# Sixteen tiles of y loaded ahead of the second pass, twelve of them into other rings

## The chip, the cores and the metric

One core of a Trainium2 chip runs the kernel. The metric is the device time of one execution in microseconds (us), the median of several runs. Lower is better.

## What is computed

x is a tensor of 2048 images x 512 channels x 8 x 8, float32. Two layers follow each other, each on a group norm of its input (32 groups of 16 channels, statistics per image):

```python
x = x + L0(_gn(x))      # L0: each channel's 8x8 block is mixed by one 64x64 matrix, plus a bias
x = x + L1(_gn(x))

def L1(x):
    h = sign(batchnorm(x, bn1_gamma, bn1_beta))          # over images and positions, per channel
    bw = sign(conv_w) * scale_of(conv_w)
    h = conv3x3(h, bw, groups=16)
    h = batchnorm(h, bn2_gamma, bn2_beta) + x
    return where(h > 0, h, prelu_a * h)
```

The two batch norms need sums over all 2048 images before anything can go on. They cut the kernel into three passes over the data.

## The kernel before, in words

**Tiles.** x is taken in B = 128 units of 16 images: 128 partitions (4 images x 32 groups) x 4096 floats, 2 MB. Pass 1 makes y, the group-normed input of the second layer, and writes it to y_scratch in DRAM. Pass 2 reads y again in T2 = 256 tiles of 32 images x 128 channels (partitions are channels there), takes the signs, convolves, and writes the integer sums h, packed two to a word, to h_scratch. Pass 3 (T3 = 128 tiles) reads y and h and writes out.

**Engines.** Each engine runs its own list of instructions, written out by hand; semaphores join them. Every transfer is issued by SyncE (the block at L313), in the order of its list. `rounds` (L281) writes out the first tiles of a pass, then a hardware loop of four tiles a turn, then four tiles more. `i, c` is the round and the place in it; tile t is `SLOTS * i + c`.

**Pass 1.** Per unit and quarter TensorE turns ring_x (L1002), ScalarE copies the turned values to ring_gT (L577) and takes mean and square of x with ring_g as a place to throw the values (L584, L590), TensorE mixes (L1016, L1019; semaphore mixed), VectorE adds x and puts z in ring_z (L764, evicted) and counts it (L773, z_counted), GpSimd normalises z into ring_y (L481, y_done), and SyncE stores ring_y (store_y, L338).

**Between the passes.** VectorE, TensorE and GpSimd turn the sums into the scale and shift of the first batch norm, bn1 (L805 to L831, bn1_ready). The pair has to change its layout from 32 groups to 128 channels, so SyncE writes it to DRAM (L372, bn1_out) and reads it back (L375, bn1_in), 4 KB each. The first sign (L632) waits for bn1_in. SyncE has by then loaded the first four tiles of y into ring_x (L365), between the stores of y of units 125 and 126.

**Pass 2.** ScalarE signs a tile (take_sign, L626, two activations L632), VectorE packs two halves into one frame (L840), TensorE convolves with 18 matmuls (L1084), ScalarE unpacks two tiles later (L637, L643) into one of four word slots, VectorE counts h (L848) and every 16 tiles sums up (L855), SyncE stores the word slot (store_h, L380, L383). A y tile is 1 MB in two transfers of 512 KB (load_y2, L354, L359), rows of 1 KB; an h tile is one transfer of 512 KB. There are four y slots, all in ring_x:

```python
            def pass2(i, c):
                t = SLOTS * i + c
                if until(i, c, T2 - SLOTS):
                    sp.wait_ge(signed, 2 * t + 2)
                    load_y2(i, c + SLOTS)
                if from_round(i, c, 3):
                    store_h(i, c - 3)
```

ring_z, ring_y, ring_g and ring_gT aren't used in pass 2; pass 3 uses them for y and h from its first loads on (load_3, L396).

Of the kernel before, what the change touches and what calls it, by code (L numbers as in the profile page):

```python
# [18 lines left out]
SIDE = 8  # L19
J = C // P  # L20
NQ = 4
# [3 lines left out]
FU = NQ * SL  # L25
UNIT = NQ * (P // GROUPS)
BANK = 512
PAIRS = GC // 2
HEAD = TAIL = 4
SLOTS = 4  # L30
# [4 lines left out]
IMG = 16  # L35
# [21 lines left out]
def two_layer_kernel(nc, x, w0, b0, conv_w, g1, be1, g2, be2, prelu_a, ident_in, quarter_in, clif_in, pick_in, out):  # L57
    N = x.shape[0]
    B = N // UNIT
    T2 = (B // 2) * J  # L60
# [13 lines left out]
    y_chan = y_dram.rearrange("b (m k c f) -> b k c m f", m=4, k=J, c=P)  # L74
# [3 lines left out]
    with ExitStack() as ctx:  # L78
        def sb(name, shape, dt=F32):
            return ctx.enter_context(nc.sbuf_tensor(name, shape, dt))  # L80

        def sem(name):
            return ctx.enter_context(nc.semaphore(name))

        ring_x = sb("ring_x", [P, SLOTS, FU])
        ring_z = sb("ring_z", [P, 2, FU])
        ring_y = sb("ring_y", [P, 2, FU])
        ring_g = sb("ring_g", [P, SLOTS, SL])
        ring_gT = sb("ring_gT", [P, SLOTS, SL])
        late = sb("late", [P, 2, 2048])  # L90
        early = sb("early", [P, GC * P])
# [84 lines left out]
        def y2_slot(s):  # L176
            return ring_x[:, s // 2, 2048 * (s % 2):2048 * (s % 2) + 2048]

        def word_slot(s):
            return ring_x[:, 2, 1024 * s:1024 * s + 1024].bitcast(I32)  # L180

# [13 lines left out]
        def relu_slot(m):  # L195
            return late[:, m // 4, BANK * (m % 4):BANK * (m % 4 + 1)]

        def sum_bank(m):
            return h_acc[m // 2][:, BANK * (m % 2):BANK * (m % 2 + 1)]

# [24 lines left out]
        x_squared = sem("x_squared")  # L225
# [6 lines left out]
        mixed = sem("mixed")  # L232
        evicted = sem("evicted")
        z_counted = sem("z_counted")
# [5 lines left out]
        y_stored = [sem(f"y_stored{s}") for s in range(2)]  # L240
# [9 lines left out]
        bn1_in = sem("bn1_in")  # L250

        y2_loaded = [sem(f"y2_loaded{s}") for s in range(SLOTS)]
        signed = sem("signed")
        packed = sem("packed")
        conv_done = sem("conv_done")
# [25 lines left out]
        def rounds(eng, body, total, head=HEAD):  # L281

            loops = (total - head - TAIL) // SLOTS
            for c in range(head):
                body(0, c)
            with eng.Fori(0, loops) as i:
                for c in range(head, head + SLOTS):
                    body(i, c)
            for c in range(head, head + TAIL):
                body(loops, c)  # L290

        def from_round(i, c, n):

            return not (isinstance(i, int) and SLOTS * i + c < n)

        def until(i, c, n):

            return not (isinstance(i, int) and SLOTS * i + c >= n)

        def row(ap, b):  # L300
            if isinstance(b, int):
                return ap[b]
            one = ap[bass.ds(b, 1)]
            return one.rearrange("a p f -> (a p) f") if len(one.shape) == 3 else one.rearrange(
                "a p n f -> (a p) n f")
# [8 lines left out]
        def _(sp):  # L314
# [23 lines left out]
            def store_y(i, c):  # L338
                b = SLOTS * i + c
                sp.wait_ge(y_done, 4 * b + 4)  # L340
                sp.dma_start(row(y_unit, b), ring_y[:, c % 2, :]).then_inc(y_stored[c % 2], 16)
# [11 lines left out]

            def load_y2(i, c):  # L354

                s = c % SLOTS
                pair = 2 * (i + c // J)
                for e in range(2):
                    sp.dma_start(y2_slot(s)[:, 1024 * e:1024 * (e + 1)].rearrange("p (m f) -> p m f", m=4),  # L359
                                 row(y_chan[:, c % J], pair + e)).then_inc(y2_loaded[s], 16)  # L360

            sp.wait_ge(evicted, 4 * (B - 2))
            sp.wait_ge(y_stored[0], 16)
            sp.wait_ge(y_stored[1], 16)
            for c in range(SLOTS):  # L365
                load_y2(0, c)
            loops1 = (B - SLOTS) // SLOTS
            store_y(loops1, SLOTS - 2)
            store_y(loops1, SLOTS - 1)

            sp.wait_ge(bn1_ready, 1)
            sp.dma_start(bn1_dram.rearrange("(q j) s -> q (j s)", j=GC),  # L372
# [3 lines left out]
                         allow_slow_non_contiguous=True).then_inc(bn1_in, 16)  # L376
            for s in range(2):
                sp.wait_ge(y_stored[s], 16 * (B // 2))

            def store_h(i, c):  # L380
                t = SLOTS * i + c
                sp.wait_ge(unpacked, t + 1)
                sp.dma_start(row(h_chan[:, c % J], i + c // J),  # L383
                             word_slot(c % SLOTS).rearrange("p (m f) -> p m f", m=4)).then_inc(h_stored[c % SLOTS], 16)

            def pass2(i, c):
                t = SLOTS * i + c
                if until(i, c, T2 - SLOTS):
                    sp.wait_ge(signed, 2 * t + 2)
                    load_y2(i, c + SLOTS)  # L390
                if from_round(i, c, 3):
                    store_h(i, c - 3)

            rounds(sp, pass2, T2, 2 * HEAD)

            def load_3(i, c):  # L396

# [161 lines left out]
        def _(act):  # L559
# [65 lines left out]

            def take_sign(i, c):  # L626
                t, s = SLOTS * i + c, c % SLOTS
                act.wait_ge(y2_loaded[s], 32 * (i + c // SLOTS + 1))
                if from_round(i, c, 2):
                    act.wait_ge(packed, t - 1)  # L630
                for e in range(2):
                    act.activation(  # L632
                        sign_slot(c % 2)[:, e].rearrange("p (a n b) -> p n a b", a=SIDE, n=IMG),
                        y2_slot(s)[:, 1024 * e:1024 * (e + 1)].rearrange("p (n a b) -> p n a b", n=IMG, a=SIDE),
                        ACT.Sign, bias=bn1_c[:, c % J, 1:2], scale=bn1_c[:, c % J, 0:1]).then_inc(signed, 1)

            def unpack(i, c):  # L637
# [13 lines left out]
                if from_round(i, c, 2):  # L651
                    unpack(i, c - 2)

            rounds(act, pass2, T2, 2 * HEAD)
            last = (T2 - SLOTS) // SLOTS
            unpack(last, SLOTS - 2)
            unpack(last, SLOTS - 1)
# [33 lines left out]
        def _(dve):  # L691
# [56 lines left out]
            for n in range(NQ):  # L748
                dve.tensor_scalar(rank_rhs[:, n, :].rearrange("p (r f) -> p r f", f=S),
                                  part.unsqueeze(1).to_broadcast([P, BANK // S, S]), pick[:, 5 + n:6 + n], None,  # L750
                                  ALU.mult).then_inc(rank_ready, 1)
# [15 lines left out]
            def z_stat(i, c, j):  # L767
# [3 lines left out]
                dve.wait_ge(evicted, 4 * (SLOTS * i + c) + j + 1)  # L771
                for r in range(PAIRS):
                    last = dve.bn_stats(z_tup[:, s, j, 2 * r:2 * r + 2, :].rearrange("p h t -> p (h t)"),  # L773
# [69 lines left out]
            def h_stat(i, c):  # L843
# [3 lines left out]
                for q in range(4):  # L847
                    last = dve.bn_stats(h_tup[:, c % J, c // J, q, :], parts[:, BANK * q:BANK * (q + 1)])  # L848
                last.then_inc(h_counted, 1)
# [142 lines left out]
        def _(pe):  # L992
            def turn(i, c, j):
# [5 lines left out]
                if from_round(i, c, 1) or j >= 2:  # L999
                    pe.wait_ge(gT_done, step - 1)  # L1000
                for r in range(PAIRS):
                    last = pe.transpose(psT[:, j % 2, P * r:P * (r + 1)],  # L1002
# [8 lines left out]
            def product(i, c, j):  # L1011
# [3 lines left out]
                for h in range(2):  # L1015
                    pe.matmul(psV[:, j % 2, BANK * h:BANK * (h + 1)], rank_lhs[:, c % 2, :], rank_rhs[:, j, :],  # L1016
                              start=True, stop=False)
# [126 lines left out]
```

## Time and profile before

| | us |
|---|---|
| runs, median of 3 | 4591.73 (4591.44 to 4593.64) |
| the profiled execution, its own time | 4591.19 |
| its span in the profile | 4589.1 |
| TensorE matmuls busy | 4297.1 |
| VectorE busy | 4173.0 |
| ScalarE busy | 3861.6 |
| GpSimd busy | 1476.0 |

The profile is of one execution; all times in it count from the start of its span. Pass 1 ends near 1751, pass 2 runs from 1761 to about 2805. The transfers moved 1612.18 MB. Busy time is not the same as being the limit: an engine can be busy 90% of the time and still wait for something each turn. The DMA share is the mean busy share of the 16 DMA engines; in this profile it goes a little over 1 where they are full. "To landing" is the time from the issue of a transfer to its last byte. SPq is the queue of SyncE, that is, the time it spends on issuing transfers.

### The profile page before, as it was taken

The page shows a single profiled execution, that of the slowest core. Times are in us where ns is not written, and L with a number is a line of the kernel's source. Part 1 is how long each engine was busy: PE and PEld are TensorE (multiplying, and loading weights), DVE is VectorE, ACT ScalarE, POOL GpSimd, SP SyncE. Part 2 cuts the span into 40 slices and gives each one's busy share as a digit, 9 for nine tenths or more (in the row PEclk, how much of TensorE's full clock was granted, in tenths as well). Part 3 has the DMA queues.
Part 4 walks back from the last instruction along what each step waited for, and adds up shares of the span by engine and source line. Part 5 has one row for each costly group of instructions (what it writes and reads, how often), then busy time and mean ns, then how long its engine had stood idle before and what let it go on. Part 6 is the DMA issues. An engine that isn't in the chain of part 4 may idle for free.

```text
span 4589.1 us, 82259 instructions
## 1 busy us (share of the span) xinstructions
PE 4297.1 (94%) x21948; PEld 2702.5 (59%) x21948; DVE 4173.0 (91%) x9963; ACT 3861.6 (84%) x5517; POOL 1476.0 (32%) x3480
## 2 busy tenths in 40 slices
PE   6999999999999997999999995999999999999998
PEld 6999999999999994444444442444444444444443
DVE  6999999999999997999899987999999999999998
ACT  7999999999999995888888885777777777777776
POOL 3888888888888883000000000000000000000000
PEclk9999999999999998999999998999999999999999
DMA  5888888888888889999999997999999999999998
GB/s 198 317 318 320 316 316 323 314 319 322 316 317 318 320 302 315 385 385 385 385 385 385 385 385 289 383 389 388 389 387 386 390 387 389 387 388 387 388 387 308
DMA packets 686230, 1612.18 MB, mean 351 GB/s; under 512 B 30002, under 2 KB 423986, under 8 KB 620658
## 3 DMA queue, kind: packets, MB, share of 16 engines
q1 hardware_dynamic: 686194, 1611.76, 95.7%
q8 instruction: 16, 0.26, 0.0%
q14 instruction: 20, 0.16, 0.0%
HBM read 940.55 MB, written 671.10 MB: 351 GB/s over the span
## 4 chain that ended last, share of the span: by engine, by line
PE 51%; SPq 20%; ACT 11%; DVE 9%; issue 8%; DMA 1%; DVEq 0%; ACTq 0%; POOL 0%
PE psV L1019 17%; SPq L359 12%; PE psT L1002 10%; DVE ring_x L958 8%; SPq L383 7%; PE psT L1104 5%; PE psV L1016 5%; PE psT L1106 5%; PE psV L1106 4%; PE psV L1104 4%; ACT ring_y L678 3%; ACT ring_z L678 3%; ACT ring_g L584 2%; PE psV L1100 1%; ACT late L668 1%
## 5 line engine op out<-in xcount | busy, mean ns | idle before, releaser
L1019 PEld LDWEIGHTS psV<-W0T,ring_gT 128*128 128x128 f32 x8192 | 1077.0, 192 | 33.7
L1019 PE MATMUL psV<-W0T,ring_gT 128*128 128x128 f32 x8192 | 1080.2, 275 | 0.0
L773 DVE BATCH_NORM_STATS2 early<-ring_z 128x6 f32<-128x128 f32 x4096 | 822.6, 274 | 0.0
L764 DVE SCALAR_TENSOR_TENSOR ring_z<-psV,x_r,ring_x 128x1024 f32<-128x1024 f32 x512 | 657.3, 1284 | 117.6 <-DVE early L773 76.9
L668 ACT ACTIVATE late<-ring_x,minus_b 128x512 f32<-128x512 f32 x1024 | 639.6, 707 | 0.9 <-PE psV L1106 0.9
L848 DVE BATCH_NORM_STATS2 h_tup<-ring_x 128x6 f32<-128x512 uint16 x1024 | 630.7, 678 | 0.5
L632 ACT ACTIVATE ring_x<-ring_x,bn_c 128x1024 f16<-128x1024 f32 x512 | 604.1, 1230 | 31.0 <-DMA bn_c<-bn_scratch 31.0
L481 POOL TENSOR_SCALAR ring_y<-ring_z,u_r,u_nm 128x1024 f32<-128x1024 f32 x512 | 605.7, 1199 | 35.6 <-POOL gn L500 35.6
L590 ACT ACTIVATE ring_g<-ring_x,x_ms 128x1024 f32<-128x1024 f32 x512 | 585.2, 1143 | 0.0
L577 ACT ACTIVATE ring_gT<-psT 128x1024 f32<-128x1024 f32 x512 | 523.7, 1023 | 49.2 <-PE psT L1002 23.7
L678 ACT ACTIVATE ring_y<-ring_y,gnb 128x512 f32<-128x512 f32 x512 | 368.1, 801 | 211.2 <-DVE ring_x L958 175.7
L1084 PE MATMUL psT<-late 128*128 128x448 f16 (+3 forms) x2304 | 480.5, 364 | 67.0 <-DVE late L840 66.9
L1002 PE MATMUL psT<-ident,ring_x 128*128 128x128 f32 x4096 | 538.8, 275 | 3.9 <-ACT rank_lhs L596 0.4
L584 ACT ACTIVATE ring_g<-ring_x 128x1024 f32<-128x1024 f32 x512 | 536.9, 1049 | 0.0
L678 ACT ACTIVATE ring_z<-ring_z,gnb 128x512 f32<-128x512 f32 x512 | 368.1, 801 | 190.2 <-DVE ring_x L958 190.2
L1106 PE MATMUL psT<-late,early 128*128 128x512 f32 x1024 | 523.8, 593 | 0.0
L1084 PE MATMUL psV<-late 128*128 128x448 f16 (+3 forms) x2304 | 475.5, 362 | 31.4 <-DVE late L840 31.4
L976 DVE SCALAR_TENSOR_TENSOR ring_x<-ring_x,bn_q,psV 128x512 f32<-128x512 f32 x512 | 374.3, 744 | 117.5 <-PE psV L1106 90.3
L1002 PEld LDWEIGHTS psT<-ident,ring_x 128*128 128x128 f32 x4096 | 458.9, 141 | 26.3 <-ACT rank_lhs L596 25.5
L1084 PEld LDWEIGHTS psT<-late 128*128 128x128 f16 x2304 | 216.2, 98 | 330.7 <-issue 88.8
L1016 PE MATMUL psV<-early,rank_lhs 128*128 128x512 bf16 x1024 | 389.1, 380 | 19.6 <-ACT ring_gT L577 5.5
L840 DVE SCALAR_TENSOR_TENSOR late<-ring_x 128x1024 f16<-128x1024 f16 x256 | 312.9, 1222 | 102.5 <-ACT ring_x L632 92.8
(153 smaller groups left out, 5682.8 us busy)
## 6 DMA issues: line engine op xcount, KB each, us to landing
ring_x<-in_x SPq DMA_DIRECT2D x128, 2048.0 KB, 8.8
y_scratch<-ring_y SPq DMA_DIRECT2D x128, 2048.0 KB, 12.8
ring_x<-y_scratch SPq DMA_DIRECT2D x512, 512.0 KB, 7.6
out<-ring_x SPq DMA_DIRECT2D x256, 1024.0 KB, 14.4
h_scratch<-ring_x SPq DMA_DIRECT2D x256, 512.0 KB, 7.8
ring_y<-y_scratch SPq DMA_DIRECT2D x128, 1024.0 KB, 8.1
ring_z<-y_scratch SPq DMA_DIRECT2D x128, 1024.0 KB, 8.2
ring_g<-h_scratch SPq DMA_DIRECT2D x64, 1024.0 KB, 12.2
```

The lines of the kernel that those rows point to most:

```text
L481: pool.tensor_scalar(ring_y[:, c % 2, :].rearrange("p (r n s) -> p n r s", r=GC, n=NQ)[:, j], ring_z[:, c % 2, SL * j:SL * (j + 1)].rearra ...
L584: act.activation(ring_g[:, 2 * (j % 2), :], ring_x[:, s, SL * j:SL * (j + 1)], ACT.Copy, scale=-1.0 / (SL * ROOT), accum_out=x_ms[:, s, 0, ...
L668: act.activation(relu_slot(m), t_slot(c % 2)[:, m], ACT.Relu, bias=minus_b2[:, ch:ch + 1], scale=-1.0).then_inc(relu_done, 1)
L678: last = act.activation(v, v, ACT.Identity, bias=gnb[:, s, e, 0, n:n + 1], scale=gnb[:, s, e, 1, n:n + 1])
L764: dve.scalar_tensor_tensor(out=ring_z[:, c % 2, cols], in0=psV[:, j % 2, :], scalar=x_r[:, s, j:j + 1], in1=ring_x[:, s, cols], op0=ALU.mu ...
L773: last = dve.bn_stats(z_tup[:, s, j, 2 * r:2 * r + 2, :].rearrange("p h t -> p (h t)"), ring_z[:, c % 2, SL * j + 2 * S * r:SL * j + 2 * S ...
L848: last = dve.bn_stats(h_tup[:, c % J, c // J, q, :], parts[:, BANK * q:BANK * (q + 1)])
L1002: last = pe.transpose(psT[:, j % 2, P * r:P * (r + 1)], ring_x[:, s, SL * j + P * r:SL * j + P * (r + 1)], ident[:, :])
L1016: pe.matmul(psV[:, j % 2, BANK * h:BANK * (h + 1)], rank_lhs[:, c % 2, :], rank_rhs[:, j, :], start=True, stop=False)
L1019: last = pe.matmul(psV[:, j % 2, P * r:P * (r + 1)], ring_gT[:, j, P * r:P * (r + 1)], W0T[:, :], start=False, stop=(r % 4 == 3))
L1084: last = pe.matmul(sums[:, IMG * a.start:IMG * a.stop, b.start:b.stop], conv_wT[:, c % J, tap, :], rows[:, IMG * (a.start + dy):IMG * (a.s ...
L1106: pe.matmul(sum_bank(m), diag[:, 8 * (c % 2) + m, :], relu_slot(m), start=False, stop=True).then_inc(combined, 1)
```

## The change

SyncE loads tiles 0 to 3 as before. Behind them it loads tiles 4 and 5 into ring_g once the last square of x is done, 6 and 7 into ring_gT once the last product is done, then stores units 126 and 127, loads tiles 8 to 11 into ring_z once the last z is counted and stored, does the two bn1 transfers, and loads tiles 12 to 15 into ring_y. In the pass, tile t = 0 to 3 is followed by the load of tile t + 16 into its slot in ring_x, tiles 4 to 15 by none, and from tile 16 on t is followed by t + 4, as before. The twelve early tiles have semaphores of their own.

```diff
+AHEAD = 16
...
+        def y2_place(i, c):
+
+            if not (isinstance(i, int) and SLOTS <= SLOTS * i + c < AHEAD):
+                return y2_slot(c % SLOTS)
+            n = SLOTS * i + c - SLOTS
+            if n < SLOTS:
+                return (ring_g if n < 2 else ring_gT)[:, 2 * (n % 2):2 * (n % 2) + 2, :].rearrange("p s f -> p (s f)")
+            return (ring_z if n < 2 * SLOTS else ring_y)[:, :, :].rearrange("p s f -> p (s f)")[
+                :, 2048 * (n % SLOTS):2048 * (n % SLOTS) + 2048]
...
+        y2_early = [sem(f"y2_early{t}") for t in range(SLOTS, AHEAD)]
...
             def load_y2(i, c):
 
-                s = c % SLOTS
+                early = isinstance(i, int) and SLOTS <= SLOTS * i + c < AHEAD
+                loaded = y2_early[SLOTS * i + c - SLOTS] if early else y2_loaded[c % SLOTS]
                 pair = 2 * (i + c // J)
                 for e in range(2):
-                    sp.dma_start(y2_slot(s)[:, 1024 * e:1024 * (e + 1)].rearrange("p (m f) -> p m f", m=4),
-                                 row(y_chan[:, c % J], pair + e)).then_inc(y2_loaded[s], 16)
+                    sp.dma_start(y2_place(i, c)[:, 1024 * e:1024 * (e + 1)].rearrange("p (m f) -> p m f", m=4),
+                                 row(y_chan[:, c % J], pair + e)).then_inc(loaded, 16)
 
             sp.wait_ge(evicted, 4 * (B - 2))
-            sp.wait_ge(y_stored[0], 16)
-            sp.wait_ge(y_stored[1], 16)
+            for s in range(2):
+                sp.wait_ge(y_stored[s], 16 * (AHEAD // J))
             for c in range(SLOTS):
                 load_y2(0, c)
             loops1 = (B - SLOTS) // SLOTS
+            sp.wait_ge(x_squared, NQ * B)
+            load_y2(1, 0)
+            load_y2(1, 1)
+            sp.wait_ge(mixed, NQ * B)
+            load_y2(1, 2)
+            load_y2(1, 3)
             store_y(loops1, SLOTS - 2)
             store_y(loops1, SLOTS - 1)
+            sp.wait_ge(z_counted, NQ * B)
+            for c in range(SLOTS):
+                load_y2(2, c)
 
             sp.wait_ge(bn1_ready, 1)
...
             for s in range(2):
                 sp.wait_ge(y_stored[s], 16 * (B // 2))
+            for c in range(SLOTS):
+                load_y2(3, c)
...
             def pass2(i, c):
                 t = SLOTS * i + c
                 if until(i, c, T2 - SLOTS):
-                    sp.wait_ge(signed, 2 * t + 2)
-                    load_y2(i, c + SLOTS)
+                    if not from_round(i, c, SLOTS):
+                        sp.wait_ge(signed, 2 * t + 2)
+                        load_y2(i, c + AHEAD)
+                    elif from_round(i, c, AHEAD):
+                        sp.wait_ge(signed, 2 * t + 2)
+                        load_y2(i, c + SLOTS)
                 if from_round(i, c, 3):
                     store_h(i, c - 3)
 
-            rounds(sp, pass2, T2, 2 * HEAD)
+            rounds(sp, pass2, T2, AHEAD)
...
             def take_sign(i, c):
                 t, s = SLOTS * i + c, c % SLOTS
-                act.wait_ge(y2_loaded[s], 32 * (i + c // SLOTS + 1))
+                if not from_round(i, c, SLOTS):
+                    act.wait_ge(y2_loaded[s], 32)
+                elif not from_round(i, c, AHEAD):
+                    act.wait_ge(y2_early[t - SLOTS], 32)
+                else:
+                    act.wait_ge(y2_loaded[s], 32 * (i + c // SLOTS + 2 - AHEAD // SLOTS))
...
-            rounds(act, pass2, T2, 2 * HEAD)
+            rounds(act, pass2, T2, AHEAD)
```

SyncE's order from the end of pass 1 to the first stores of h, before (a row is one kind of transfer, "waits" names the semaphores ahead of it; ring_x<-y_scratch are y tiles, two transfers each):

```order
L341 DMA y_scratch<-ring_y 128x4096 [waits y_done] x4
L359 DMA ring_x<-y_scratch 128x4x256 [waits y_stored1,y_stored0,evicted]
L359 DMA ring_x<-y_scratch 128x4x256 x7
L341 DMA y_scratch<-ring_y 128x4096 [waits y_done] x2
L372 DMA bn_scratch<-bn_q 32x32 [waits bn1_ready]
L375 DMA bn_c<-bn_scratch 128x4x2 [waits bn1_out]
L359 DMA ring_x<-y_scratch 128x4x256 [waits signed,y_stored1,y_stored0]
L359 DMA ring_x<-y_scratch 128x4x256
```

Between the last two y stores and the bn1 transfers nothing stands.

The same place in the changed kernel (the line numbers are its own; L372 is load_y2, L353 store_y, L394 and L397 the bn1 transfers):

```order
L353 DMA y_scratch<-ring_y 128x4096 [waits y_done] x4
L372 DMA ring_x<-y_scratch 128x4x256 [waits y_stored1,y_stored0,evicted]
L372 DMA ring_x<-y_scratch 128x4x256 x7
L372 DMA ring_g<-y_scratch 128x4x256 [waits x_squared]
L372 DMA ring_g<-y_scratch 128x4x256 x3
L372 DMA ring_gT<-y_scratch 128x4x256 [waits mixed]
L372 DMA ring_gT<-y_scratch 128x4x256 x3
L353 DMA y_scratch<-ring_y 128x4096 [waits y_done] x2
L372 DMA ring_z<-y_scratch 128x4x256 [waits z_counted]
L372 DMA ring_z<-y_scratch 128x4x256 x7
L394 DMA bn_scratch<-bn_q 32x32 [waits bn1_ready]
L397 DMA bn_c<-bn_scratch 128x4x2 [waits bn1_out]
```

Eight transfers now stand ahead of the last two y stores, and eight more ahead of the bn1 transfers.

Behind the bn1 transfers, before the hardware loop of pass 2, in the changed kernel:

```order
L372 DMA ring_y<-y_scratch 128x4x256 [waits y_stored1,y_stored0]
L372 DMA ring_y<-y_scratch 128x4x256 x7
L372 DMA ring_x<-y_scratch 128x4x256 [waits signed]
L372 DMA ring_x<-y_scratch 128x4x256
L372 DMA ring_x<-y_scratch 128x4x256 [waits signed]
L372 DMA ring_x<-y_scratch 128x4x256
L372 DMA ring_x<-y_scratch 128x4x256 [waits signed]
L372 DMA ring_x<-y_scratch 128x4x256
L372 DMA ring_x<-y_scratch 128x4x256 [waits signed]
L372 DMA ring_x<-y_scratch 128x4x256
L407 DMA h_scratch<-ring_x 128x4x256 [waits unpacked] x13
```

Sixteen transfers of y stand ahead of the first store of h where eight stood, and then thirteen stores of h follow with no load between them.

## Rows read from the trace of the kernel before

**Rows 1.** The page's chain that ended last, whole span, by engine and by line
```profile
PE 51%; SPq 20%; ACT 11%; DVE 9%; issue 8%; DMA 1%; DVEq 0%; ACTq 0%; POOL 0%
PE psV L1019 17%; SPq L359 12%; PE psT L1002 10%; DVE ring_x L958 8%; SPq L383 7%; PE psT L1104 5%; PE psV L1016 5%; PE psT L1106 5%; PE psV L1106 4%; PE psV L1104 4%; ACT ring_y L678 3%; ACT ring_z L678 3%; ACT ring_g L584 2%; PE psV L1100 1%; ACT late L668 1%
```

**Rows 2.** Busy time by windows in the second pass
```profile
core 0: us, PE busy (x) PEld busy (x) DVE busy (x) ACT busy (x) POOL busy (x), PEclk, DMA share, GB/s
1850.00:2750.00 900.00, 820.51 (x3972) 372.50 (x3971) 818.23 (x1221) 723.03 (x662) 0.00 (x0) 1.00 1.09 385
...
1850.00:1900.00 50.00, 46.22 (x226) 21.05 (x225) 44.61 (x63) 40.15 (x38) 0.00 (x0) 1.00 1.09 385
...
2650.00:2700.00 50.00, 45.02 (x218) 20.40 (x219) 45.52 (x70) 40.36 (x38) 0.00 (x0) 1.00 1.09 385
```

**Rows 3.** Who waited for whom, 1850 to 2750 us
```profile
engine line waited for: us in total, times, longest us
ACT ring_x L643 <- DMA h_scratch<-ring_x: 171.0, 212, 1.0
```

**Rows 4.** ScalarE's timeline, end of pass 1 and start of pass 2
```profile
start us, us, engine line op out<-in xcount [idle before <-releaser]
1711.47 1.15 ACT L590 ACTIVATE ring_g<-ring_x,x_ms 128x1024 f32<-128x1024 f32 x1
...
1761.19 6.90 ACT L632 ACTIVATE ring_x<-ring_x,bn_c 128x1024 f16<-128x1024 f32 x6 [31.04 <-DMA bn_c<-bn_scratch]
...
1772.05 2.36 ACT L632 ACTIVATE ring_x<-ring_x,bn_c 128x1024 f16<-128x1024 f32 x2
...
1775.62 2.36 ACT L632 ACTIVATE ring_x<-ring_x,bn_c 128x1024 f16<-128x1024 f32 x2
...
1785.41 1.02 ACT L643 ACTIVATE ring_x<-psT 128x1024 int32<-128x1024 f32 x1 [0.29 <-PE psT L1084]
...
1800.77 2.36 ACT L632 ACTIVATE ring_x<-ring_x,bn_c 128x1024 f16<-128x1024 f32 x2
...
1857.77 2.36 ACT L632 ACTIVATE ring_x<-ring_x,bn_c 128x1024 f16<-128x1024 f32 x2
```

**Rows 5.** Timelines of VectorE and TensorE in the first tiles of pass 2
```profile
1778.34 1.23 DVE L840 SCALAR_TENSOR_TENSOR late<-ring_x 128x1024 f16<-128x1024 f16 x1
...
1803.33 1.22 DVE L840 SCALAR_TENSOR_TENSOR late<-ring_x 128x1024 f16<-128x1024 f16 x1
...
1781.64 7.30 PE L1084 MATMUL psT<-late 128*128 128x512 f16 x36
1788.78 7.30 PE L1084 MATMUL psV<-late 128*128 128x512 f16 x36
```

**Rows 6.** The chain of waits between the passes, 1726 to 1762 us
```profile
1730.42 0.91 PE psV L1019 x8
...
1738.12 3.08 DVE early L773 x16
...
1757.66 0.19 DVE bn_q L831
1757.87 1.35 DMA bn_scratch<-bn_q
1759.24 1.93 DMA bn_c<-bn_scratch
```

**Rows 7.** SyncE's timeline: transfers issued between the passes (start, time to issue)
```profile
1726.60 0.33 SPq L341 DMA_DIRECT2D y_scratch<-ring_y  x1
...
1727.05 12.74 SPq L359 DMA_DIRECT2D ring_x<-y_scratch  x8
...
1740.22 1.02 SPq L341 DMA_DIRECT2D y_scratch<-ring_y  x1
...
1751.13 0.36 SPq L341 DMA_DIRECT2D y_scratch<-ring_y  x1
...
1763.65 11.70 SPq L359 DMA_DIRECT2D ring_x<-y_scratch  x8
```

**Rows 8.** Busy time by windows between the passes
```profile
1732.00:1734.00 2.00, 2.00 (x18) 1.91 (x16) 1.96 (x9) 0.00 (x0) 1.92 (x7) 1.00 0.85 196
1734.00:1744.00 10.00, 0.14 (x2) 0.00 (x0) 7.76 (x30) 0.00 (x0) 9.00 (x20) 0.75 1.10 357
1744.00:1750.00 6.00, 0.00 (x0) 0.00 (x0) 3.37 (x7) 0.00 (x0) 5.84 (x13) 0.50 1.07 427
1750.00:1752.00 2.00, 0.18 (x1) 0.18 (x2) 1.63 (x5) 0.00 (x0) 1.11 (x1) 0.50 0.12 49
...
1758.00:1764.00 6.00, 0.00 (x0) 0.00 (x0) 0.40 (x1) 2.81 (x3) 6.00 (x11) 0.50 0.05 1
1764.00:1766.00 2.00, 0.97 (x3) 0.43 (x4) 1.02 (x2) 2.00 (x3) 2.00 (x4) 0.50 0.53 95
...
1768.00:1770.00 2.00, 2.00 (x6) 0.69 (x5) 0.00 (x0) 0.10 (x1) 0.13 (x1) 0.55 1.09 351
```

**Rows 9.** L359 issued 1726-1740 and at 1763.65; L383 issued 1774-1790: time to landing
```profile
DMA to landing us min/median/max: 8.6/10.2/11.0
...
DMA to landing us min/median/max: 3.9/3.9/3.9
...
DMA to landing us min/median/max: 6.2/6.9/9.4
```

**Rows 10.** VectorE's sums over four tiles, groups of 1850 to 2780 us
```profile
L855 DVE BATCH_NORM_AGGREGATE h_agg<-h_tup 128x2 f32<-128x48 f32 x112 | 27.7, 319 | 0.0
```

More of the change, by code:

```diff
@@ L633, in take_sign @@
                         sign_slot(c % 2)[:, e].rearrange("p (a n b) -> p n a b", a=SIDE, n=IMG),
-                        y2_slot(s)[:, 1024 * e:1024 * (e + 1)].rearrange("p (n a b) -> p n a b", n=IMG, a=SIDE),
+                        y2_place(i, c)[:, 1024 * e:1024 * (e + 1)].rearrange("p (n a b) -> p n a b", n=IMG, a=SIDE),
                         ACT.Sign, bias=bn1_c[:, c % J, 1:2], scale=bn1_c[:, c % J, 0:1]).then_inc(signed, 1)
```

## The prediction

> **What bounds the kernel now.** I read the page first. Its chain of waits [rows 1] names TensorE and, next, the issuing queue of SyncE with the y loads of the second pass (L359); so the second pass hangs on transfers, not on an engine. The windows view of it [rows 2] shows why: over 900 us the 16 DMA engines are at a share of 1.09 and move a constant 385 GB/s, while TensorE is busy for 820.51 us and VectorE for 818.23, both about 91%. The waits of the same stretch [rows 3] say where it is felt: ScalarE's unpack (L643) waits 171.0 us, in 212 pieces, for the store of h that frees its word slot. Nobody waits for a y load. One tile loads 1.049 MB and stores 0.524 MB; 1.573 MB at 385 GB/s is 4.09 us.
>
> The pass doesn't start at that pace. In ScalarE's timeline [rows 4] tile 0 is signed from 1761.19 (the last bn1 transfer has landed), tile 3 at 1772.05, tile 4 at 1775.62, tile 11 at 1800.77 and tile 25 at 1857.77. So tiles 4 to 11 come every (1800.77 - 1775.62) / 7 = 3.59 us, later ones every (1857.77 - 1800.77) / 14 = 4.07. The 3.57 is the engines' own pace: VectorE packs tile 4 at 1778.34 and tile 11 at 1803.33 without a gap, 25.0 / 7 = 3.57, and 36 matmuls, two tiles, start 7.14 us apart [rows 5]. **The most that any early load can give is thus 4.07 - 3.57 = 0.50 us per tile**, and only while it lasts.
>
> Between the passes the chain [rows 6] runs through VectorE's last counts, GpSimd's and VectorE's small bn1 steps, and from 1757.87 two small transfers of 1.35 and 1.93 us, which SyncE issues and which hold back the first sign. SyncE's own timeline [rows 7]: the store of unit 125 at 1726.60, eight loads (four tiles) from 1727.05 to 1739.79, the stores of units 126 and 127 at 1740.22 and 1751.13, then bn1. The windows [rows 8] show the DMA engines full until 1750 (357 GB/s in loads alone, 427 while the store is in), nearly idle in 1750 to 1752, and idle from 1758 to 1764. The idle time is what the change wants to fill. It is short, some 10 us, and four tiles take 4.19 MB / 0.357 = 11.7 us. Where SyncE's rows stand in the new order is shown with the change.
>
> **The change part by part.** Four parts matter.
>
> (a) Eight tiles (1,0) to (2,3) stand in SyncE's order ahead of the bn1 transfers, the first four ahead of the last two y stores as well. Their own waits end early: the last square ends at 1712.6 [rows 4], the last product at 1731.3 and the last count at 1741.2 [rows 6], all before SyncE gets to the loads behind them. SyncE doesn't run ahead freely: its eight issues took 12.74 us in a full queue [rows 7], and loads landed 8.6 to 11.0 us after issue there, against 3.9 in an empty queue [rows 9]. So I take one line of transfers, served in turn. Before, the four tiles have drained at about 1744, when the rate rises [rows 8]. Add four tiles, 11.7: 1755.7. The two stores, 2.10 MB each at 427 GB/s, 4.9 each: 1765.5 (the last became ready at 1751.1, so it costs no wait). Four more tiles, 11.7: 1777.2. bn1 has been ready since 1757.9 [rows 6]; its write lands 1.35 after what lies before it, its read 1.93 and a few hundredths later: the first sign at 1780.5 instead of 1761.2. **Cost: 19.3 us**, on the path, because every engine waits for bn1 here. Bounds: if the loads ran at the 427 GB/s of the store's window and the bn1 write overlapped the last load, 14.1 (2 x 1.9 and 1.35 less); if each change between loads and stores cost about a microsecond more, as the 196 GB/s of 1732 to 1734 suggests [rows 8], 22. I take 19.3, from the rates of the same kinds of transfer.
>
> That a queue is served in turn is also in the Trainium skill, page "DMA: Bandwidth & Descriptors", section "Two DMAs through the same engine are not ordered": within one queue of an engine descriptors start in order. It speaks against this change. The loads' landing times of 8.6 to 11.0 us agree; whether a 4 KB transfer is held up too, no row of before shows.
>
> (b) Tiles 12 to 15 are issued after the bn1 read and before anything of pass 2, and then tiles 16 to 19, each after a sign; only then the store of h of tile 0. Before, four tiles stood there. Now 8.39 MB at 0.357 take 23.5 us. The first load before was issued at 1763.65 and the rate was full at 1766 [rows 7, 8], 2.3 later; now the issue is 1.6 before the first sign, so the flow starts at T + 0.8 (T is the first sign) and ends at T + 24.3. The store of tile 0, 0.524 MB at 385 GB/s, lands at T + 25.7. ScalarE's unpack of tile 4, which needs that slot, started at T + 24.2 [rows 4]. **Cost: 1.5 us**, on the path, since VectorE had no slack behind it [rows 5]. Bounds 0 and 5 (the 351 GB/s of a single 2 us window [rows 8], and a landing as late as the 6.9 us median of the first four h stores [rows 9]).
>
> (c) Gain. Tiles 4 to 15 now find their data there, and no load is issued while they run, because the later loads go only into the four slots of ring_x. So tile 16 stands where tile 4 stood before: four tiles in store, queue empty. Until there 12 tiles go at 3.57 instead of 12 tiles that, later on, cost 4.07. **Gain: 12 x 0.50 = 6.0 us.** The queue is idle for most of that: 12 stores, 6.3 MB, 16 us of 43. Bounds: 8.0 if the whole 16 tiles count; 3.3 if VectorE's sums after tile 19 (8 BN_AGGR of 319 ns and a copy, 2.7 us [rows 10]) aren't hidden.
>
> (d) The rest costs nothing. The waits on x_squared, mixed and z_counted are over when SyncE arrives; the store of unit 126 goes out at about 1751 instead of 1740, but nothing needs ring_y until pass 2's loads. ScalarE has 16 tiles written out instead of 8: the same activations. Pass 3 is untouched.
>
> Sum: 19.3 + 1.5 - 6.0 = +14.8. The profiled execution took 4591.19 us (span 4589.1), 0.5 below the median of 4591.73, so it may stand for the runs: 4591.73 + 14.8 = **4606.5 us**, 0.32% slower. About 0.2%, 9.2 us, is what a measurement of this kernel can tell from no change.
>
> A second rule of that page, section "Specifications", puts HBM at some 358 GB/s per core. By it the later tiles would take 1.573 / 0.358 = 4.39 us, the gain would be 9.9 and the sum +10.9. The trace disagrees, with 385 GB/s over 900 us, and the measurement decides.
>
> **Rivals.**
> *The small transfers pass the queue.* The bn1 write then lands 1.35 us after its issue. SyncE gets to it when the last load is issued, 8.6 to 11.0 us before 1777.2, so about 1768; the first sign comes at 1771 to 1772, 10 us late. But the loads still have to drain: the h store of tile 0 lands behind the same bytes, only 4.1 us sooner than in the forecast (1777.2 + 23.5 + 1.4 = 1802.1), and the unpack of tile 4, ready at 1771.5 + 24.2, waits 6.4 us for it. Sum 10.3 + 6.4 - 6.0 = +10.7: 4602. For it: the small size. Against it: SyncE's one queue.
> *Bytes decide.* If pass 2 lasted as long as its bytes at 385 GB/s from the first sign, the eight tiles that are no longer loaded in it would save 8 x 2.72 = 21.8 us: 19.3 + 1.5 - 21.8 = -1, 4591, no change. The trace of before speaks against it: tiles 4 to 11 don't beat 3.57 us although DMA is not yet the limit. The Trainium skill's same page, "Rules for kernel authors", says to issue a transfer early and wait for it late; by that rule alone the early loads are free, which is the saving of this case.
> *Another steady pace* (the faster side). If the 4.07 us came not from the DMA engines but from how loads and stores follow each other in SyncE's line, a start with full slots and no store outstanding could keep a better rhythm. Place: tiles 24 to 255. It decides from a pace 0.10 us shorter on, since (14.8 + 9.2) / 232 = 0.10; with 3.57 plus 2.7 / 16 for the sums, 3.74, it would be 4606.5 - 232 x 0.33 = 4530. Against it: a share of 1.09 and 385 GB/s, the same at the start and at the end of the 900 us [rows 2].
> *A deeper stall of the h stores*: (b) at its upper end and (a) at 21: 4612.
>
> **How the numbers follow.** Forecast 0.72; passing the queue 0.06; bytes decide 0.09; another pace 0.08; deeper stall 0.05. The forecast's bounds give +6 (14.1 + 0 - 8.0) to +23.7 (22 + 5 - 3.3); not all ends meet, and I take +6 to +22, with 0.06 of its 0.72 below +9.2. The range is 4597 to 4614: it leaves out bytes decide and another pace (0.17) and little else. Slower by over 0.2%: 0.66 + 0.06 + 0.05 = 0.77. Within: 0.09 + 0.06 = 0.15. Faster: 0.08.
>
> **What would show it.** In the profile of the changed kernel: the bn1 write issued at about 1768 or later and landing only near 1778, not 1.35 us after 1757.9; the first sign (L632's counterpart) near 1780; a wait of 1 to 5 us at the unpack of tile 4; tiles 4 to about 23 every 3.57 us; a window of some 25 us with the DMA share well below 1; then 385 GB/s and 4.07 us per tile to the end, and a third pass of the same length. A first sign before 1775, or a later pace below 4.0 us, would prove me wrong.

## The result, and the profile after

| | before | changed |
|---|---|---|
| median of the runs, us | 4591.66 | 4608.47 (4607.25 to 4609.88) |
| ratio, 95% interval | | 1.0036 (1.0025 to 1.0046) |
| span of the profiled execution | 4589.1 | 4605.2 |

The change costs 16.8 us, 0.37%. Forecast were 14.8 us and 4606.5. Lines of code below are those of the changed kernel: L372 is load_y2, L394 and L397 the bn1 transfers, L407 the store of h, L665 the sign, L676 the unpack, L873 VectorE's pack.

SyncE's timeline between the passes (start, time to issue), which answers to [rows 7]:

```profile
1726.51 12.77 SPq L372 DMA_DIRECT2D ring_x<-y_scratch  x8
1739.72 5.35 SPq L372 DMA_DIRECT2D ring_g<-y_scratch  x4
1745.12 6.16 SPq L372 DMA_DIRECT2D ring_gT<-y_scratch  x4
1751.32 1.89 SPq L353 DMA_DIRECT2D y_scratch<-ring_y  x2
1753.26 19.61 SPq L372 DMA_DIRECT2D ring_z<-y_scratch  x8
1772.92 1.41 SPq L394 DMA_DIRECT2D bn_scratch<-bn_q  x1
1780.32 0.38 SPq L397 DMA_DIRECT2D bn_c<-bn_scratch  x1
1780.80 8.44 SPq L372 DMA_DIRECT2D ring_y<-y_scratch  x8
1789.29 12.15 SPq L372 DMA_DIRECT2D ring_x<-y_scratch  x8
1801.48 36.02 SPq L407 DMA_DIRECT2D h_scratch<-ring_x  x13
```

SyncE is stuck in the issue of the tiles for ring_z when bn1 becomes ready (1757.9 before). It gets to the bn1 write at 1772.92. The chain of waits of the changed kernel, the place that answers to [rows 6] (start, duration):

```profile
1772.92 7.38 DMA bn_scratch<-bn_q
1780.30 0.02 issue
1780.32 1.92 DMA bn_c<-bn_scratch
1782.24 0.02 issue
1782.26 2.38 ACT ring_x L665 x2
```

The write takes 7.38 us, not 1.35. It lands at 1780.30, right behind the last load, which was issued at 1771.46 and took 8.7 us to land: it doesn't pass the loads that were issued before it. The read, alone in the queue, takes 1.92 as before. ScalarE's timeline, the start of pass 2, against [rows 4]:

```profile
1782.26 6.90 ACT L665 ACTIVATE ring_x<-ring_x,bn_c 128x1024 f16<-128x1024 f32 x6 [52.66 <-DMA bn_c<-bn_scratch]
...
1803.11 2.36 ACT L665 ACTIVATE ring_x<-ring_gT,bn_c 128x1024 f16<-128x1024 f32 x2
1809.84 1.02 ACT L676 ACTIVATE ring_x<-psT 128x1024 int32<-128x1024 f32 x1 [4.37 <-PE psT L1117]
1810.76 2.36 ACT L665 ACTIVATE ring_x<-ring_gT,bn_c 128x1024 f16<-128x1024 f32 x2
...
1829.85 2.36 ACT L665 ACTIVATE ring_x<-ring_y,bn_c 128x1024 f16<-128x1024 f32 x2
...
1840.56 2.36 ACT L665 ACTIVATE ring_x<-ring_x,bn_c 128x1024 f16<-128x1024 f32 x2
...
1888.43 1.02 ACT L676 ACTIVATE ring_x<-psV 128x1024 int32<-128x1024 f32 x1 [0.69 <-DMA h_scratch<-ring_x]
```

The first sign is 21.1 us late. The row at 1809.84 is the unpack of tile 4, which waits 4.37 us. The profile names TensorE as the releaser, but with fewer loads ahead of the first store of h this unpack starts 23.9 us after the first sign (the last but one experiment), which would be 1806.2. The other semaphore of the wait is that of the first store of h, which was issued at 1801.48 and took 8.3 us to land: 1809.8, just when the unpack starts. Tile 7 is signed at 1810.76 and tile 13 at 1829.85, 3.18 us a tile: ScalarE works off what TensorE has already done, and makes up 2.3 us. Then tiles go at 3.57 to tile 16 (1840.56). Only at 1888.43 does a wait for a store of h come back.

Windows between and in the passes (the last three columns are the granted clock, the DMA share and GB/s), against [rows 2, 8]:

```profile
1744.00:1756.00 12.00, 1.22 (x4) 1.00 (x4) 5.69 (x15) 0.00 (x0) 8.89 (x12) 0.50 1.10 349
...
1780.00:1782.00 2.00, 0.00 (x0) 0.00 (x0) 0.00 (x0) 0.00 (x0) 0.00 (x0) 0.50 0.15 5
...
1812.00:1840.00 28.00, 26.43 (x135) 12.85 (x134) 26.85 (x38) 27.14 (x26) 0.00 (x0) 1.00 0.50 170
1840.00:1850.00 10.00, 10.00 (x52) 4.89 (x51) 10.00 (x16) 9.35 (x9) 0.00 (x0) 1.00 0.55 179
...
1870.00:2770.00 900.00, 823.29 (x3993) 375.00 (x3991) 821.67 (x1232) 725.13 (x663) 0.00 (x0) 1.00 1.09 385
```

The DMA engines are full while everybody waits for bn1, and at about half load for the 38 us in which the tiles loaded ahead are worked off. At 385 GB/s they would have moved 8.1 MB more in these 38 us, which is 21 us of their time. After that the pass is what it was, 385 GB/s at a share of 1.09. Pass 2 ends 15.4 us late: the bn2 write that follows it is issued here, before and after.

```profile
2828.21 0.37 SPq L415 DMA_DIRECT2D bn_scratch<-bn_c  x1
```

```profile
2843.61 0.37 SPq L443 DMA_DIRECT2D bn_scratch<-bn_c  x1
```

The 0.7 us left of the 16.1 between the spans lie behind the bn2 write, and are not explained.

### The profile page after: what moved, and what is told of

Read it like the earlier page. It is cut to its first block, busy times and chain, and to the rows that moved or that the text cites. A ratio compares the mean times of both kernels' runs of the same rounds, so it can differ in the third digit from the quotient of the medians.

```text
span 4605.2 us, 81925 instructions
## 1 busy us (share of the span) xinstructions
PE 4257.1 (92%) x21692; PEld 2702.9 (59%) x21948; DVE 4171.2 (91%) x9963; ACT 3861.8 (84%) x5517; POOL 1479.6 (32%) x3480
## 4 chain that ended last, share of the span: by engine, by line
PE 21%; SPq 19%; POOL 18%; DVE 15%; issue 15%; ACT 8%; DMA 1%; POOLq 1%; DVEq 1%; ACTq 0%
SPq L372 12%; DVE ring_x L991 8%; SPq L407 6%; POOL ring_y L509 6%; PE psT L1137 5%; PE psT L1139 5%; PE psV L1137 4%; PE psV L1139 4%; DVE early L806 4%; ACT ring_y L711 3%; ACT ring_z L711 3%; POOL u_r L523 2%; POOL x_r L485 2%; DVE ring_z L797 2%; PE psV L1133 1%
## 5 line engine op out<-in xcount | busy, mean ns | idle before, releaser
L665 ACT ACTIVATE ring_x<-ring_x,bn_c 128x1024 f16<-128x1024 f32 x488 | 575.8, 1230 | 52.8 <-DMA bn_c<-bn_scratch 52.7
L873 DVE SCALAR_TENSOR_TENSOR late<-ring_x 128x1024 f16<-128x1024 f16 x256 | 312.5, 1221 | 120.0 <-ACT ring_x L665 110.8
L1139 PE MATMUL psV<-late,early 128*128 128x512 f32 x768 | 392.2, 592 | 0.0
```

Of the source, the lines that this page charges most:

```text
L665: act.activation(sign_slot(c % 2)[:, e].rearrange("p (a n b) -> p n a b", a=SIDE, n=IMG), y2_place(i, c)[:, 1024 * e:1024 * (e + 1)].rearr ...
L1139: pe.matmul(sum_bank(m), diag[:, 8 * (c % 2) + m, :], relu_slot(m), start=False, stop=True).then_inc(combined, 1)
```

## The experiments

The theory after the result: while the DMA engines are the limit of pass 2, only the bytes that they don't move count, whatever the reason (no load issued, an empty queue). (All transfers of y and h in pass 2 are of 512 KB, so bytes can't be told from the number of transfers here.) Three rivals: the late bn1 is a loss by itself (A); a small transfer is held up by the full DMA engines, whichever queue it comes from (B); the pace of 4.07 us is a rhythm of SyncE's list (C).

The ratios compare each kernel with the kernel before, run beside it. The median of the kernel before was 4591.66 us beside the change and 4592.51 to 4592.71 beside the experiments, so a difference of 1 to 2 us between an experiment and the change isn't much more than this drift. Where it matters the time of the bn2 write in the profiles is given too.

**The bn1 transfers issued by ScalarE**

```diff
-            sp.wait_ge(bn1_ready, 1)
-            sp.dma_start(bn1_dram.rearrange("(q j) s -> q (j s)", j=GC),
...
-            sp.wait_ge(bn1_out, 16)
-            sp.dma_start(bn1_c[:, :, :], bn1_dram.rearrange("(k p) s -> p k s", p=P),
...
+            act.wait_ge(bn1_ready, 1)
+            act.dma_start(bn1_dram.rearrange("(q j) s -> q (j s)", j=GC),
...
+            act.wait_ge(bn1_out, 16)
+            act.dma_start(bn1_c[:, :, :], bn1_dram.rearrange("(k p) s -> p k s", p=P),
             act.wait_ge(bn1_in, 16)
```

> The change, but the two bn1 transfers are issued by ScalarE, so they don't stand in SyncE's line. Theory (bytes in line): what costs is the bytes that stand ahead of the first store of h; the first sign then comes near 1763 us, not 1782, but the unpack of tile 4 still waits for a store that lands near 1804, some 18 us instead of 4. Only the few us in which the DMA engines idle around bn1 come back: about 4603. Rival A (the late bn1 is itself the loss): nearly all of the 21 us come back, 4588. Rival B (a transfer of another queue waits behind the full DMA engines all the same): first sign after 1775, 4607.

Measured: 4606.2 us, ratio to before 1.0029 (1.0018 to 1.0041). ScalarE's timeline of this kernel (L659 is the sign, L670 the unpack):

```profile
1758.58 0.36 ACTq L675 DMA_DIRECT2D bn_scratch<-bn_q  x1
1763.98 0.40 ACTq L678 DMA_DIRECT2D bn_c<-bn_scratch  x1
1771.07 6.91 ACT L659 ACTIVATE ring_x<-ring_x,bn_c 128x1024 f16<-128x1024 f32 x6 [40.26 <-DMA bn_c<-bn_scratch]
...
1807.13 1.02 ACT L670 ACTIVATE ring_x<-psT 128x1024 int32<-128x1024 f32 x1 [12.97 <-issue]
```

The first sign comes 11.2 us sooner than in the change, and 8.5 us of that are lost again at the unpack of tile 4, with 12.97 us of waiting. A falls: of the 21 us 2.3 came back by the medians, and in the profiles the bn2 write is 0.7 us earlier. B is half right: beside full DMA engines the two small transfers took 5.4 and 7.1 us, against 1.35 and 1.93 alone [rows 6]. The first sign came 8 us later than the theory had it (1763), the total 3.2 us above its 4603 and nearer to B's 4607. As a small transfer is slow in a queue of its own too, the 7.38 us of the change don't tell the turn in SyncE's queue from the full engines.

**All twelve tiles behind the bn1 transfers**

```diff
-            sp.wait_ge(x_squared, NQ * B)
-            load_y2(1, 0)
...
-            for c in range(SLOTS):
-                load_y2(2, c)
...
-            for c in range(SLOTS):
-                load_y2(3, c)
+            for n in range(1, 4):
+                for c in range(SLOTS):
+                    load_y2(n, c)
```

> The change, but tiles 4 to 11 are loaded behind the bn1 transfers too, with tiles 12 to 15. Theory (bytes in line): the first sign is back at 1761, but sixteen tiles (16 x 3.0 us) stand ahead of the first store of h, which lands near 1812; the unpack of tile 4 waits about 27 us and the total is 4611, as slow as the change. Rival A (the late bn1 is the loss): 4591.7 + 4 - 6, about 4590.

Measured: 4611.76 us, ratio 1.0043 (1.0026 to 1.0060). Its first sign and its unpack of tile 4:

```profile
1761.11 6.90 ACT L657 ACTIVATE ring_x<-ring_x,bn_c 128x1024 f16<-128x1024 f32 x6 [31.01 <-DMA bn_c<-bn_scratch]
...
1812.85 1.02 ACT L668 ACTIVATE ring_x<-psT 128x1024 int32<-128x1024 f32 x1 [28.04 <-issue]
```

The clearest of the runs: 4611 and 27 us were expected, 4590 by rival A. The first sign comes when it did before (1761.11), and the kernel is the slowest of all. The same twelve tiles stand ahead of the first store of h instead of bn1, and the wait is 28.04 us there.

**Four tiles instead of twelve**

```diff
-AHEAD = 16
+AHEAD = 8
...
-            sp.wait_ge(z_counted, NQ * B)
-            for c in range(SLOTS):
-                load_y2(2, c)
...
-            for c in range(SLOTS):
-                load_y2(3, c)
```

> Eight tiles ahead instead of sixteen: only tiles 4 to 7, into ring_g and ring_gT, in the place where the change has its first four. Theory: the line is 12 us longer, bn1 waits for the last y store, first sign near 1769.5 (+8); the first h store stands behind no more than before, so unpack of tile 4 doesn't wait; four tiles at 0.5 us are gained: 4597 to 4598. Rival A expects the same here; if the gain is 2.7 us a tile (bytes decide), 4589.

Measured: 4599.39 us, ratio 1.0016 (1.0006 to 1.0026). The loss shrinks to 6.9 us, 1.4 us more than the upper end of what was expected. For four tiles used up in a row 2.7 us a tile (4589) is excluded. The first sign came at 1771.83, 2 us later than expected, because the bn1 write stood 11.0 us behind two y stores:

```profile
1758.90 0.33 SPq L391 DMA_DIRECT2D bn_scratch<-bn_q  x1
1769.94 0.39 SPq L394 DMA_DIRECT2D bn_c<-bn_scratch  x1
```

**The same sixteen tiles, used up slowly.** The sixteen slots are kept in turn, and one load in about nine is left out, each time one for a slot outside ring_x, until four slots are left. `LOAD[t]` is the tile loaded after tile t, and from tile SPREAD (112) on t is followed by t + 4 in the four slots.

```diff
                 if until(i, c, T2 - SLOTS):
-                    if not from_round(i, c, SLOTS):
-                        sp.wait_ge(signed, 2 * t + 2)
-                        load_y2(i, c + AHEAD)
-                    elif from_round(i, c, AHEAD):
+                    if from_round(i, c, SPREAD):
                         sp.wait_ge(signed, 2 * t + 2)
                         load_y2(i, c + SLOTS)
+                    elif t in LOAD:
+                        sp.wait_ge(signed, 2 * t + 2)
+                        load_y2(0, LOAD[t])
```

> The change, but the loads that are left out are not those after tiles 4 to 15 in a row: one in about nine is left out (after tiles 8, 20, 26, 35, 48, 53, 62, 71, 80, 89, 100, 111), so that the DMA engines never idle and the engines' own pace (3.57, 3.74 with the sums) never binds. Theory (bytes decide once the DMA engines are kept full): each tile loaded ahead is then worth 1.049 MB / 385 GB/s = 2.72 us instead of 0.5, 12 x 2.2 = 26 us better than the change: 4582, 10 us faster than before. Rival C (the 4.07 us pace comes from the rhythm of SyncE's list, or the gain is bound to tiles and not to bytes): 4605 to 4609.

Measured: 4587.87 us, ratio 0.9990 (0.9981 to 1.0000). Nothing ahead of the first sign differs from the change (it came at 1782.92), and the kernel is 20.6 us faster than the change, about 4.6 us faster than before, at the edge of the interval. C as it was put, 4605 or more, falls. Three of its windows:

```profile
1810.00:1860.00 50.00, 46.47 (x229) 21.58 (x228) 43.25 (x61) 41.96 (x39) 0.00 (x0) 1.00 1.09 384
1860.00:1910.00 50.00, 47.73 (x239) 22.85 (x238) 48.83 (x76) 43.60 (x42) 0.00 (x0) 1.00 1.09 385
...
2450.00:2750.00 300.00, 273.71 (x1325) 124.07 (x1323) 272.30 (x410) 241.35 (x221) 0.00 (x0) 1.00 1.09 385
```

While loads are left out VectorE is busy for 48.83 of 50 us instead of some 45 [rows 2], at the same 385 GB/s: the engines do more tiles with the same bytes. It was 6 us short of what I had expected, 26 us better than the change. What was regained is the half load of the change, which is gone here (384 GB/s from 1810 to 1860 against 170 and 179 from 1812 to 1850), and that was worth 21 us. Another way to count it gives nearly the same, but is only an argument: tiles 12 to 15 are loaded after the bn1 read, so only eight of the twelve come off what pass 2 has to move, 8 x 2.72 = 21.8.

That SyncE's own issuing sets the pace can be ruled out as well. In the change, at half load of the DMA engines, the three transfers of a tile are issued in 1.4 us, far less than 4.07:

```profile
1843.12 0.99 SPq L372 DMA_DIRECT2D ring_x<-y_scratch  x2
1844.39 0.40 SPq L407 DMA_DIRECT2D h_scratch<-ring_x  x1
```

**The two together**

```diff
+            act.wait_ge(bn1_ready, 1)
+            act.dma_start(bn1_dram.rearrange("(q j) s -> q (j s)", j=GC),
...
```

> e4_spread with the two bn1 transfers issued by ScalarE. Theory (only the idle time of the DMA engines counts once nothing else binds): the first sign comes 11 us sooner, as in e1_bn1_act, but only the 3 us that the DMA engines idled around bn1 come back: 4585. If the first sign counted, 4577.

Measured: 4585.48 us, ratio 0.9984 (0.9974 to 0.9993). The first sign came at 1770.76, 12 us sooner than without the edit, and 2.4 us came back (2.9 at the bn2 write), as expected.

**Four tiles in the idle stretch behind bn1, used up slowly**

```diff
-AHEAD = 16
+AHEAD = 8
...
+            for c in range(SLOTS):
+                load_y2(1, c)
```

> Eight tiles ahead, tiles 4 to 7 loaded right behind the bn1 transfers (SyncE issues bn1), one load in about eight left out (after tiles 12, 20, 27, 38), so that the four are used up slowly. Theory: the first sign stays at 1761, the DMA engines are full from 1762 instead of 1766 and don't empty near 1776; 6 to 7 us of idle time filled: 4586. If a tile ahead were worth its 2.72 us whatever it costs to load, 4581.

Measured: 4587.56 us, ratio 0.9988 (0.9979 to 0.9998). That is 1.6 us more than expected. By the medians four tiles in the right place are worth as much as twelve in the spread kernel above (4587.87); in the profiles the bn2 write comes 1.2 us later than there.

**Four tiles behind the last y store, bn1 issued by ScalarE**

AHEAD and the loads left out are those of the last kernel.

```diff
             store_y(loops1, SLOTS - 1)
+            for c in range(SLOTS):
+                load_y2(1, c)
...
+            act.wait_ge(bn1_ready, 1)
+            act.dma_start(bn1_dram.rearrange("(q j) s -> q (j s)", j=GC),
...
```

> As e6_four_spread, but the four tiles stand right behind the last y store, and ScalarE issues the bn1 transfers. Theory: the DMA engines are also filled from 1757 to 1762; the first sign comes a few us later (two transfers among full engines), which costs nothing: 4582 to 4583. If the late first sign counts, 4590.

Measured: 4589.59 us, ratio 0.9992 (0.9983 to 1.0002). A miss by 7 us, at what was given for the case that the late first sign counts (4590), and an instructive one:

```profile
1763.15 1.41 SPq L396 DMA_DIRECT2D ring_gT<-y_scratch  x1
1773.34 4.84 SPq L396 DMA_DIRECT2D ring_x<-y_scratch  x5
```

SyncE had nothing to issue for 9 us, since the next load waits for the first sign, and the sign came only at 1770.89: the bn1 transfers took 5.2 and 6.7 us beside the four tiles. The windows of this kernel show the gap (219 GB/s):

```profile
1762.00:1766.00 4.00, 0.00 (x0) 0.00 (x0) 0.00 (x0) 0.00 (x0) 4.00 (x8) 0.50 1.10 349
1766.00:1774.00 8.00, 0.00 (x0) 0.00 (x0) 0.71 (x1) 3.11 (x3) 1.48 (x3) 0.50 0.76 219
```

So a late sign does cost, where SyncE runs dry because of it.

**Eight tiles in that place**

Against the kernel above:

```diff
-AHEAD = 8
-SKIPS = [12, 20, 27, 38]
-SPREAD = 40
+AHEAD = 12
+SKIPS = [8, 17, 27, 37, 46, 54, 62, 72]
+SPREAD = 76
...
+            for c in range(SLOTS):
+                load_y2(2, c)
```

> As e7_four_act with twelve tiles ahead, tiles 4 to 11 behind the last y store, eight loads left out one in nine. Theory: no idle time is left to fill beyond that of e7_four_act, so four more tiles give nothing; loads alone run at 350 GB/s and mixed with stores at 385, which takes 1 us: 4583 to 4584. If more tiles ahead were worth more, 4575 or less.

Measured: 4585.40 us, ratio 0.9985 (0.9975 to 0.9994). I had expected nothing from four more tiles, because I had not foreseen the gap of the last kernel. They gave 4.2 us, and they fill just that gap (336 GB/s from 1766 to 1774); they give nothing over the kernel with twelve tiles, bn1 by ScalarE and slow use (4585.48).

**The first stores of h ahead of tiles 16 to 19**

```diff
-                    if not from_round(i, c, SLOTS):
+                    if isinstance(t, int) and 8 <= t < 12:
                         sp.wait_ge(signed, 2 * t + 2)
-                        load_y2(i, c + AHEAD)
+                        load_y2(i, c + AHEAD - 8)
```

> The change, but tiles 16 to 19 are loaded after the signs of tiles 8 to 11, not 0 to 3, so that only eight transfers stand ahead of the first store of h behind bn1. Theory: the first sign stays at 1782, the 4.4 us wait at the unpack of tile 4 goes; but ScalarE made up some 2.5 us of it afterwards (3.17 us a tile for six tiles), so only 1.5 to 2 us come back: 4606.5 to 4607. If the wait counted in full: 4604.

Measured: 4606.79 us, ratio 1.0031 (1.0018 to 1.0043), 1.7 us less than the change. The unpack of tile 4 waits 0.29 us here, so the wait of 4.4 us had cost about that. In the profiles the bn2 write isn't earlier (2843.78 against 2843.61), but the first sign is 1.4 us later (1783.68 against 1782.26); counted from the first sign 1.3 us came back. The amount is uncertain by the drift of about 1 us, but it is below the 4.

**The loads left out one in four.** Against the kernel with one in nine:

```diff
-SKIPS = [8, 20, 26, 35, 48, 53, 62, 71, 80, 89, 100, 111]
-SPREAD = 112
+SKIPS = [8, 12, 20, 21, 24, 28, 34, 36, 44, 45, 52, 53]
+SPREAD = 56
```

> e4_spread with the twelve loads left out closer together, one in about four, between tiles 8 and 53 (8, 12, 20, 21, 24, 28, 34, 36, 44, 45, 52, 53). Theory: 48 tiles would take the DMA engines 3.40 us each, but the engines need 3.57 and 3.74 with VectorE's sums, so the DMA engines idle again and 10 to 16 us of e4_spread's gain are lost: 4598 to 4604. If only the number of tiles loaded ahead counted, 4588.

Measured: 4596.87 us, ratio 1.0010 (1.0000 to 1.0019), 9.0 us more than with one in nine, where 10 to 16 were expected. A window in it:

```profile
1950.00:2000.00 50.00, 48.63 (x246) 23.70 (x245) 49.53 (x78) 44.30 (x41) 0.00 (x0) 1.00 1.03 347
```

VectorE is busy for 49.53 of 50 us and the DMA engines move 347 GB/s: the engines are the limit there.

**One row for all.** If only missing bytes count, the GB/s moved between 1726 and 1900 us tell where pass 2 ends, since from 1900 on nearly all the kernels move 385. This is bookkeeping, not a forecast: the GB/s come from each kernel's own profile. It holds because the rate is the same in all of them afterwards. The window of before and that of the change:

```profile
1726.00:1900.00 174.00, 136.98 (x687) 67.98 (x686) 141.79 (x245) 116.02 (x107) 34.65 (x64) 0.91 1.00 350
```

```profile
1726.00:1900.00 174.00, 119.13 (x610) 61.31 (x610) 125.77 (x224) 103.14 (x95) 32.44 (x64) 0.85 0.93 316
```

174 us x (350 - 316) / 385 = 15.4 us later; the bn2 write is 15.4 us later. The same sum for the others (the windows' GB/s, the time of the bn2 write in the profile):

| kernel | GB/s | worked out, us | bn2 write | bn2 write against before, us |
|---|---|---|---|---|
| before | 350 | 0 | 2828.21 | 0 |
| the change | 316 | +15.4 | 2843.61 | +15.4 |
| bn1 by ScalarE | 317 | +14.9 | 2842.90 | +14.7 |
| all behind bn1 | 307 | +19.4 | 2847.98 | +19.8 |
| four tiles | 334 | +7.2 | 2835.17 | +7.0 |
| spread | 362 | -5.4 | 2823.92 | -4.3 |
| spread, bn1 by ScalarE | 370 | -9.0 | 2821.02 | -7.2 |
| four, behind bn1, spread | 358 | -3.6 | 2825.14 | -3.1 |
| four, bn1 by ScalarE, spread | 355 | -2.3 | 2826.50 | -1.7 |
| eight, bn1 by ScalarE, spread | 364 | -6.3 | 2822.82 | -5.4 |
| the first h stores ahead | 317 | +14.9 | 2843.78 | +15.6 |

One in four isn't in the table: it still runs below 385 after 1900. In the kernels that use the tiles up slowly the sum gives 0.5 to 1.8 us too much gain; why is open.

## Why the prediction was right

It held: 4606.5 forecast in 4597 to 4614, 4608.47 measured, slower as said. By its own steps:

(a) The bytes ahead of bn1: 19.3 us forecast, 21.1 measured at the first sign. Of the 1.8 us too little, 0.6 are the rate of loads alone, which was taken too high: 349 GB/s over 12 us against the 357 of one window, in whose first 2 us the engines moved 387. The write landed some 1.8 us behind the end of the loads' bytes, not 1.35 (they end near 1778.5: 164 GB/s from 1778 to 1779, 25 from 1779 to 1780). The rest isn't separated. The 4 KB write landed behind the loads (7.38 us after its issue), so the rival that it passes the queue didn't happen.

(b) The stall of the unpack of tile 4: 1.5 forecast, 4.4 measured (0.3 before). But it was wrong to put it on the path in full, "since VectorE had no slack": ScalarE made up 2.3 us in the six tiles after it. Taking the stall away gave 1.7 us by the medians, 1.3 counted from the first sign, so the 1.5 was right by luck: two errors cancel.

(c) The gain: 6.0 us forecast. Pass 2 ends 15.4 us late with a first sign 21.1 late, so 5.7 us were made up in it, after (b)'s 1.3 to 1.7; the gain was 7.0 to 7.4, above the 6.0 and inside the bounds of 3.3 and 8.0. Part of it is the start: tile 3 is signed 10.1 us after tile 0 instead of 10.9. The lower bound rests on a misread row: 112 BN_AGGR are busy for 27.7 us [rows 10], so eight take 2.0 us and not 8 x 319 ns, which changes nothing in the forecast. The stretch of low DMA share lasted 38 us, not some 25. The step that decides was right: twelve loads left out in a row gain about the difference of the two paces, 0.50 us a tile (0.6 measured), and not 2.72. The spread kernel shows with the same tiles loaded in the same places how much more they can be worth.

(d) Nothing: right, but for 0.7 us behind pass 2.

The sum of 14.8 us was 2.0 too low against the medians and 1.3 too low against the spans of the profiled executions (16.1). That is 1.8 too little in (a) and 0.7 in (d), less the 1.0 to 1.4 by which the gain in (c) was too small. So the mechanism was right, and the number came out this close because errors partly cancel.

The rival "another steady pace" is excluded by the 385 GB/s and the share of 1.09 from 1870 to 2770, the same as before. "Bytes decide" was set aside because the engines are the limit for tiles 4 to 15. That was right for this order of loads and wrong as a general statement: in the spread kernels bytes do decide, and the same early loads make the kernel faster than before.

What the prediction lacked was the common measure. It added a late first sign and a stall as two costs. The experiments show that either can be traded for the other, almost us for us: the first sign 11 us sooner gave 2.3 us (0.7 at the bn2 write), 21 us sooner cost 3.3 (4.4). What both stand for is the time in which the DMA engines moved less than 385 GB/s.

## What to carry to other kernels

In a stage that the DMA engines limit, judge an early load by whether it fills time in which they idle, and count the bytes that they don't move, not the waits: the window of GB/s over the seam between the stages accounts for the end of the pass in ten kernels to within 2 us. Data loaded ahead paid here only where it was used up so slowly that the engines didn't become the limit; twelve tiles used up in a row lost 16.8 us, the same twelve used up over 112 tiles won 4.6, at the edge of what the runs can tell. Before big loads are put into a queue, look for the small transfer on which the next stage hangs and which is issued behind them; giving it a queue of its own brought the first sign back by 11 of 21 us here, and the kernel by about 2 of 17. A late sign costs by itself where SyncE then has nothing to issue, as with four tiles behind the last y store.

## What wasn't expected of the hardware

Two 4 KB transfers, one after the other, took 1.35 and 1.93 us alone. Issued by ScalarE beside full DMA engines they took 5.1 to 5.8 and 6.7 to 7.1 us in the four kernels that do so; the write behind loads in SyncE's queue took 7.38 us. The second queue spares the wait to be issued, but didn't get them around the full engines. Loads of y alone (rows of 1 KB) ran at 348 to 350 GB/s at a share of 1.10, loads and h stores mixed at 385 at 1.09; so twelve more tiles loaded with no stores beside them cost an estimated 3 us more than in the mix: 12.6 MB at 349 instead of 385 GB/s.
